# The squares of both feature halves summed on GpSimd before the first norm's product, and ring loads and first gathers reordered

## The chip, the cores and the metric

The kernel runs on one core of one Trainium2 chip. The metric is the device time in microseconds (us) of one execution. PE is the matrix engine (TensorE), DVE the vector engine, ACT the scalar engine, POOL the GpSimd engine, and SP the engine that issues most DMAs. Each engine runs its own instructions in order; they meet at semaphores.

## The reference

4096 tokens (64 sequences of 64 tokens, 256 features) go through a conditioned adapter, attention with a window inside each sequence, and a layer of 32 experts, of which each token takes the best 4:

```
def _rmsnorm(x, w):
    rms = rsqrt(mean(x * x, axis=-1) + 1e-5)
    return w * (x * rms)
x0 = up(relu(down(x, cond)), cond) + x          # per-sequence adapter
qkv = _rmsnorm(x0, attn_norm_w) @ qkv_w + qkv_b # 16 query heads, 4 key heads of 64
x2 = x0 + attention(rope(q), rope(k), v) @ proj_w + proj_b
h2 = _rmsnorm(x2, ffn_norm_w)
topv, topi = top_k(h2 @ gate_w + gate_b, 4); gw = softmax(topv)
y2 = sum over the 4 experts of gw * ((silu(g) * u) @ W_down),  [u, g] = h2 @ W_up
out = x + x2 + y2
```

## The kernel before

Part 1 handles the tokens in eight chunks of 512 (numbered m = 0 to 7), with tokens along the free axis and the 256 features as two halves (c = 0, 1) of 128 partitions. Part 2 handles 159 tiles of 128 token-expert pairs, expert by expert. Each engine's order in part 1 is written out by hand in the table ORDERS: a start, then one text for chunk 0, one for chunks 1 to 6, one for the last. A word there is one step; `steps_of` unrolls them.

The steps of one chunk that matter here, in order:

- `up` on DVE (L1411, L1414) scales two products out of PSUM; `up` on POOL (L683, L689) adds them and the input, which gives the chunk's activations x0 in two halves; `up` on ACT (L1125) squares each half into a scratch tile, tmp[0][0] and tmp[0][1].
- `sums` on PE (L808) multiplies each squared half with a matrix of ones and accumulates both products in one PSUM bank, which leaves the sum over all 256 features in every row. ACT turns it into an inverse root (L1157, L1159), DVE multiplies x0 with it (L1469) and splits the result into an upper and a lower part (L1473).
- `pair` (five a chunk) makes query and key heads: PE L821, DVE L1486, then on POOL one subtraction and one addition (L706, L708). DVE may not write the products of a pair before POOL has finished the pair two before it.
- `split` (96 in all, twelve in most chunks) prepares the experts' weights for part 2: a third of an expert is loaded by SP (L537, L539), ACT rounds it to an upper part (L1245), POOL subtracts that to get the lower part (L724), SP stores both (L546, L547). Five buffers hold thirds, three hold upper parts.
- Routing of the chunk before: DVE picks the experts (`route_list`, L1587 to L1606, with the small product L1596 in it), ACT packs and tags rows (L1229, L1237), and `put` on POOL scatters 128 rows into an expert's list by an indirect DMA (L717).

In chunks 1 to 6 POOL's order is: four splits, a pair, three splits, two pairs, a split, two pairs, two splits, eight puts, `up`, split, put, split, seven puts.

Between the parts SP loads the first four experts into a ring of four slots (`load_expert`, L604): the first when the last stores have landed, three more when the last projection of part 1 is done. ACT waits until every put has landed, loads the first tile's rows (`load_rows`, L1328), reads the plan of the tiles, loads the rows of five more tiles, and then begins the tiles (`turn_in`, L1296). PE keeps itself busy with products that nobody reads (`unread`, L764), whose numbers stand in BUSY: 30 before the plan's small products, 40 after them. Then PE turns the rows of tile 0 and tile 1 (L1008) and starts the experts' products (L1034).

Of the kernel before, what the change touches and what calls it, by code (L numbers as in the profile page):

```python
# [55 lines left out]

ROWS_AHEAD = NG - 4
NPUT, NLATE = 2, 4
BUSY = (11, 14, 24, 14, 20, 30, 40)


NP = 4
# [10 lines left out]

ORDERS = {
    "PE": ("""
        cond down up sums pair pair pair pair pair down score up value
    """, """
        value score turn_prob score attend sums project turn_prob pair pair score attend value pair
        project value pair turn_prob pair attend down value project turn_prob score attend up
        project  # L80
    """, """
        score route_turn score turn_prob route_turn value attend sums route_turn project turn_prob
        route_turn pair pair route_pick score attend value pair route_count project pair pair value
        turn_prob value attend down project turn_prob score attend up project
    """, """
        score route_turn score turn_prob route_turn route_pick attend route_turn value project
        route_count route_turn turn_prob attend route_turn route_pick value project route_count
        turn_prob route_turn score attend value route_pick project turn_prob attend route_count
        route_turn project route_pick route_turn route_pick route_count route_count
    """),  # L90
    "DVE": ("""
        cond down relu scale up weights apply pair pair pair pair pair constants down relu softmax_a
        up softmax_b value
    """, """
        value softmax_a softmax_b apply project softmax_a pair pair softmax_b softmax_a value pair
        value project pair pair softmax_b down relu value project softmax_a up softmax_b project
    """, """
        softmax_a softmax_a value softmax_b apply project softmax_b pair pair route_pick value
        softmax_a pair route_count project pair pair value route_list value softmax_b down project
        relu softmax_a up softmax_b project  # L100
    """, """
        softmax_a softmax_a route_pick value softmax_b project route_count route_list softmax_b
        route_pick project value route_count route_list softmax_a value softmax_b project route_pick
        route_count route_list project route_pick route_count route_list route_pick route_count
        route_list
    """),
    "ACT": ("""
        cond split split down split split weights up sums apply split split split down split split
        softmax_a up
    """, """  # L110
        turn_prob split softmax_a attend split sums split split apply project split turn_prob split
        split softmax_a split attend split split turn_prob softmax_a project split attend split down
        turn_prob split project split attend split softmax_a split split project up split
    """, """
        route_turn turn_prob route_turn softmax_a attend split sums split route_turn apply softmax_a
        project turn_prob split root route_turn pack split split attend split split split project
        split route_pick pack split turn_prob softmax_a attend tag tag turn_prob down project attend
        softmax_a split split pack tag up project tag pack
    """, """
        route_turn turn_prob route_turn root softmax_a attend route_pick pack route_turn softmax_a  # L120
        root route_turn turn_prob pack tag attend pack pack project route_pick route_turn tag
        project root route_turn turn_prob tag attend softmax_a tag pack turn_prob pack route_pick
        project attend tag route_turn root project route_turn root tag route_pick pack route_pick
        pack tag tag
    """),
    "POOL": ("""
        split split split split pair split pair pair up pair pair split split split split up
    """, """
        split split split split split split split pair split split pair split pair pair pair split
        split split split split up split split split  # L130
    """, """
        split split split split pair split split split pair pair split pair pair split split put put
        put put put put put put up split put split put put put put put put put
    """, """
        put put put put put put put put put put put put put put put put put put put put put put put
        put put put put put put put
    """),
    "SP": ("""
        load_third load_x_t load_third load_middle load_third store_third store_third load_third
        store_third load_third load_third load_late load_third store_third move store_third load_x_t  # L140
        move move move move load_third store_third load_third load_third store_third load_third
        store_third store_third load_third
    """, """
        load_third load_x_t store_third load_third store_third store_third load_third load_third
        store_third store_third store_third load_third store_third load_third move load_third move
        store_third fill_before load_third load_third store_x2 store_third store_third move move
        load_third store_x2 load_third load_third move store_third store_third store_third
        store_third load_third load_third load_third store_third load_third store_x2 store_third
        load_third store_x2 store_third load_third store_third
    """, """  # L150
        load_third load_x_t store_third load_third store_third load_third store_third store_third
        load_third fill_before move load_third store_third load_third store_x2 store_third move
        store_third load_third move move store_x2 load_third move store_third load_third store_third
        load_third store_x2 store_third store_x2 load_third store_third load_third store_third
    """, """
        store_x2 store_x2 fill_before store_x2 store_x2
    """),
}

# [11 lines left out]


GROUPS = len(ROOTS)
TIMES = {"cond": 1, "scale": 1, "weights": 1, "constants": 1, "load_middle": 1, "load_late": 1, "fill_before": NM, "down": NM, "relu": NM, "up": NM, "sums": NM, "apply": NM, "pair": NM * NPAIR,
         "move": NM * NPAIR, "load_x_t": NM, "root": GROUPS, "route_pick": GROUPS, "route_count": GROUPS,
         "route_list": GROUPS, "put": NT * TOPK, "split": 3 * E, "load_third": 3 * E, "store_third": 3 * E}

# [68 lines left out]
def program(nc, d):  # L246
# [7 lines left out]
    def sem(name):  # L254
        return ctx.enter_context(nc.semaphore(name))
# [50 lines left out]
    ones = sb1("ones", [P, P])  # L306
# [15 lines left out]
    tmp = [[spare[:, 4 * i + j, :] for j in range(4)] for i in range(2)]  # L322
# [35 lines left out]
    start = prob[1][:, :, :].rearrange("p a k -> p (a k)")  # L358
# [65 lines left out]
    ident_b = ident[:, :].bitcast(BF16)[:, 0:P]  # L424

    s_vector = sem("s_vector")


    s_early, s_middle, s_late, s_fill, s_before = (sem(f"s_{n}") for n in ("early", "middle", "late", "fill", "before"))
# [76 lines left out]
    def listed(t):  # L506

        return s_listed[put_at[t]], 16 * TOPK * put_at[:t + 1].count(put_at[t])
# [8 lines left out]
    def sync_program(e):  # L517
# [99 lines left out]

        w.wait_ge(s_q_add, NPAIR * NM)
        w.wait_ge(s_proj, NT)
        for n in range(1, RING):  # L620
            load_expert(n)

# [39 lines left out]
    def gpsimd_program(e):  # L662
# [13 lines left out]
        def up(m):  # L676
# [49 lines left out]
        for name, k in steps_of("POOL"):  # L726
            if name == "up":
                up(k)
            elif name == "pair":
# [22 lines left out]
    def tensor_program(e):  # L752
# [349 lines left out]
    def scalar_program(e):  # L1102
# [794 lines left out]
```

## Time and profile before

| what | value |
|---|---|
| runs | 982.19, 980.65, 976.25 us (median 980.65) |
| profiled execution | 978.0 us |
| its span, first to last instruction | 976.0 us |
| mean granted TensorE clock | 0.979 |

The profile is of one execution: its instructions fill 976.0 us, and 2.0 us lie around them. A row gives a start in us from the span's beginning, a duration in us, an engine and a line of the kernel; a remark in square brackets at its end is the idle time before it and who ended it.

### The profile page before, as it was taken

What the parts mean: (1) busy time and instruction counts of PE and PEld (TensorE: products, weight loads), DVE (VectorE), ACT (ScalarE), POOL (GpSimd) and SP (SyncE); (2) the same over time, 40 slices, a digit from 0 to 9 for tenths busy, and PEclk for the clock granted to TensorE, in tenths of its full rate; (3) what the DMA queues carried; (4) which work ended last, traced back from release to release, by engine and by line L of the source; (5) the groups of instructions that cost most, each with busy time, mean ns of one, the idle gap of its engine ahead of it and who ended that gap; (6) DMA issues with size and microseconds to landing.
All of it is one profiled execution on the core that took longest, in us unless ns stands there. A gap on an engine that the chain in (4) does not pass through costs nothing.

```text
span 976.0 us, 21879 instructions
## 1 busy us (share of the span) xinstructions
PE 921.6 (94%) x7434; PEld 742.7 (76%) x7434; DVE 804.2 (82%) x1808; ACT 523.1 (54%) x1246; POOL 542.5 (56%) x507
## 2 busy tenths in 40 slices
PE   7989899989999999898988999999999999999998
PEld 3657676776867678676753888888888888888887
DVE  5989799999999989998864777777777877777777
ACT  3144463836557374573750666665666666566641
POOL 3647558897888778787565233433343334343340
PEclk9989999999999899999998999999999999999999
DMA  8789889798897978879249877777867759663798
GB/s 276 195 258 306 277 260 288 242 303 264 278 306 242 291 242 286 253 264 276 92 147 347 269 246 278 246 252 253 285 218 284 256 188 317 232 231 108 249 394 303
DMA packets 127447, 251.41 MB, mean 258 GB/s; under 512 B 18756, under 2 KB 66122, under 8 KB 126797
## 3 DMA queue, kind: packets, MB, share of 16 engines
q1 hardware_dynamic: 83436, 186.79, 57.8%
q0 software_dynamic: 13776, 34.64, 9.8%
q10 hardware_dynamic: 30128, 28.58, 9.6%
q8 instruction: 64, 1.05, 0.5%
q14 instruction: 43, 0.34, 0.1%
HBM read 135.64 MB, written 102.12 MB: 244 GB/s over the span
## 4 chain that ended last, share of the span: by engine, by line
PE 57%; DVE 15%; POOL 9%; issue 6%; DMA 5%; ACT 4%; SPq 3%; ACTq 0%; DVEq 0%; POOLq 0%
PE gbank L1034 11%; PE scores L1034 11%; PE scores L1053 5%; PE gbank L1053 5%; DVE ring L1486 5%; PE gbank L904 5%; POOL lists L717 5%; DMA rows_in<-lists 2%; PE gbank L1097 2%; PE gbank L821 2%; DVE entry L1596 2%; PE scores L1008 2%; PE gbank L1008 2%; PE gbank L1043 2%; PE scores L1043 2%
## 5 line engine op out<-in xcount | busy, mean ns | idle before, releaser
L739 POOL DMA_INDIRECT pick_rows<-rows_out,pair_i x159 | 158.7, 998 | 265.6 <-ACT rows_out L1310 262.2
L724 POOL TENSOR_TENSOR ring<-ring 128x512 fp32r<-128x512 f32 x96 | 123.5, 1297 | 64.1 <-ACT ring L1245 63.8
L717 POOL DMA_INDIRECT lists<-put_rows,slot_i x112 | 108.8, 972 | 54.8 <-issue 29.8
L1034 PE MATMUL scores<-ring,in_part 128*128 x480 | 132.6, 412 | 1.5 <-DVE in_part L1726 1.5
L1034 PE MATMUL gbank<-ring,in_part 128*128 x474 | 129.8, 409 | 0.0
L821 PE MATMUL gbank<-h_t,w_qk 128*128 128x512 f32 x480 | 117.8, 399 | 1.6 <-ACT ring L1189 0.7
L904 PE MATMUL gbank<-w_o,ring 128*128 128x256 f32 x512 | 116.5, 381 | 1.8 <-ACT ring L1189 1.7
L1245 ACT ACTIVATE ring<-ring 128x512 fp32r<-128x512 f32 x96 | 59.5, 627 | 108.9 <-DMA w_parts<-ring 74.6
L1486 DVE SCALAR_TENSOR_TENSOR ring<-gbank,b_qk,rope 128x512 f32<-128x512 f32 x160 | 107.9, 743 | 3.8 <-PE gbank L821 3.5
L904 PEld LDWEIGHTS gbank<-w_o,ring 128*128 128x128 f32 x512 | 95.2, 191 | 14.2 <-ACT ring L1189 2.7
L821 PEld LDWEIGHTS gbank<-h_t,w_qk 128*128 128x128 f32 x480 | 88.8, 188 | 22.6 <-ACT ring L1189 1.1
L1034 PEld LDWEIGHTS scores<-ring,in_part 128*128 128x128 f32 x480 | 85.0, 191 | 15.8 <-issue 1.7
L1034 PEld LDWEIGHTS gbank<-ring,in_part 128*128 128x128 f32 x474 | 83.2, 189 | 13.7
L1053 PEld LDWEIGHTS scores<-ring,mid_part 128*128 128x128 f32 x480 | 67.8, 189 | 7.8 <-issue 0.4
L1053 PEld LDWEIGHTS gbank<-ring,mid_part 128*128 128x128 f32 x474 | 67.0, 189 | 7.2
L1296 ACT ACTIVATE in_part<-scores,norm_w 128x128 fp32r<-128x128 f32 x160 | 50.0, 364 | 39.4 <-PE scores L1008 23.1
L1053 PE MATMUL scores<-ring,mid_part 128*128 x480 | 70.2, 282 | 0.1
L1053 PE MATMUL gbank<-ring,mid_part 128*128 x474 | 69.2, 282 | 0.0
L1734 DVE SCALAR_TENSOR_TENSOR mid<-scores,rows_in,silu 128x256 f32<-128x256 f32 x80 | 38.6, 483 | 35.3 <-ACT silu L1302 35.3
L1302 ACT ACTIVATE silu<-scores,rows_in 128x256 f32<-128x256 f32 x80 | 37.9, 473 | 51.5 <-PE scores L1034 51.2
L1734 DVE SCALAR_TENSOR_TENSOR mid<-gbank,rows_in,silu 128x256 f32<-128x256 f32 x79 | 38.1, 482 | 27.4 <-ACT silu L1302 27.4
L1302 ACT ACTIVATE silu<-gbank,rows_in 128x256 f32<-128x256 f32 x79 | 37.4, 474 | 42.1 <-PE gbank L1034 41.2
(214 smaller groups left out, 1930.2 us busy)
## 6 DMA issues: line engine op xcount, KB each, us to landing
w_parts<-ring SPq DMA_DIRECT2D x192, 256.0 KB, 4.0
ring<-w_parts SPq DMA_DIRECT2D x32, 1536.0 KB, 7.7
rows_in<-lists ACTq DMA_DIRECT2D x159, 136.0 KB, 3.8
ring<-in_W_up SPq DMA_DIRECT2D x64, 256.0 KB, 4.4
picks<-pick_rows SPq DMA_DIRECT2D x6, 2048.0 KB, 13.9
ring<-in_W_down SPq DMA_DIRECT2D x32, 256.0 KB, 4.3
q_r<-rot SPq DMA_DIRECT2D x16, 512.0 KB, 6.4
q_r<-ring SPq DMA_DIRECT2D x16, 512.0 KB, 6.7
```

What stands on the lines that cost most here:

```text
L717: e.indirect_dma_start(out=lists, out_offset=bass.IndirectOffsetOnAxis(ap=slot_i[r % NPAY][:, s * TOPK + k:s * TOPK + k + 1], axis=0), in_ ...
L724: e.tensor_tensor(lower, lower.bitcast(F32), upper.bitcast(F32), ALU.subtract).then_inc(s_lower, 1)
L739: e.indirect_dma_start(out=pick_rows, out_offset=bass.IndirectOffsetOnAxis(ap=pair_i[:, i:i + 1], axis=0), in_=rows_out[i % NY][:, :], in_ ...
L821: ins = e.matmul(bank[:, :], w_qk[:, x, c, 2 * j + o, :], h_t[i][:, y, c, :], start=k == 0, stop=k == len(CHUNK_PRODUCTS) - 1)
L904: ins = e.matmul(bank[:, 0:D], y_t[:, n // REP, n % REP, :, :].rearrange("p b s -> p (b s)"), w_o[:, n, :], start=False, stop=n == 2 * REP ...
L1034: ins = e.matmul(front[i % FRONTS], in_parts[i % IN_BUFS][x][:, c, :], ring[:, bass.ds(at + y * WE + c * 2 * DFF, 2 * DFF)], start=k == 0, ...
L1053: ins = e.matmul(out, mid_parts[i % 2][x][:, c, :], ring[:, bass.ds(at + y * WE + KC * 2 * DFF + c * D, D)], start=k == 0, stop=k == len(C ...
L1245: e.activation(w_upper[q % NU], w_third[q % NW].bitcast(F32), ACT.Copy).then_inc(s_upper, 1)
L1296: ins = e.activation(in_parts[i % IN_BUFS][0][:, c, :], front[i % FRONTS][:, c * P:(c + 1) * P], ACT.Copy, scale=norm2_w[:, c:c + 1])
L1302: e.activation(silu[i % 2][:, :], front[i % FRONTS][:, DFF:2 * DFF], ACT.Silu, scale=rows_in[i % NG][:, D + 2:D + 3]).then_inc(s_silu, 1)
L1486: e.scalar_tensor_tensor(out=by_seq(t[n][:, :]), in0=by_seq(gbank[banks[o]][:, :]), scalar=b_qk[:, 2 * j + o:2 * j + o + 1], in1=rope[:, t ...
L1734: e.scalar_tensor_tensor(out=mid[i % MID_BUFS][:, :], in0=front[i % FRONTS][:, 0:DFF], scalar=rows_in[i % NG][:, D + 2:D + 3], in1=silu[i ...
```

## The change

Four edits:

1. A new POOL step `squares` adds tmp[0][1] to tmp[0][0] once ACT has squared both halves, for chunks 1 to 7. PE's `sums` then makes one product of the sum where it made two; chunk 0 stays as it was.
2. POOL's order gets the step: right behind `up` of chunk 1; behind `up`, split, split of chunk 2; behind `up`, split, put of chunks 3 to 7 (ahead of a split and seven puts). No other word of ORDERS changes; the other lines of the table are only wrapped anew.
3. SP waits for the landing of every put before it loads experts 1 to 3 into the ring.
4. ACT begins tile 0 (`turn_in(0)`) before it loads the rows of tiles 4 and 5, where it loaded all five first. PE's unread products before the plan are 20 where they were 30.

```diff
-BUSY = (11, 14, 24, 14, 20, 30, 40)
+BUSY = (11, 14, 24, 14, 20, 20, 40)
...
     "POOL": ("""
-        split split split split pair split pair pair up pair pair split split split split split up
+                 split split split split pair split pair pair up pair pair squares split split split split split up
+        squares
     """, """
...
-        split split split split up split split split split
+        split split split split up split split squares split
     """, """
...
-        put put put put put put up split put split put put put put put put put
+        put put put put put put up split put squares split put put put put put put put
...
         w.wait_ge(s_proj, NT)
+        for t in sorted(max(u for u in range(NT) if put_at[u] == b) for b in range(NPUT + NLATE)):
+            w.wait_ge(*listed(t))
         for n in range(1, RING):
             load_expert(n)
...
+        def squares(m):
+            if m == 0:
+                return
+            w.wait_ge(s_sq, KC * (m + 1))
+            e.tensor_tensor(tmp[0][0][:, :], tmp[0][0][:, :], tmp[0][1][:, :], ALU.add).then_inc(s_sq_sum, 1)
...
-            for c in range(KC):
-                w.wait_ge(s_sq, KC * m + c + 1)
-
-                ins = e.matmul(bank[:, :], ones[:, :], tmp[0][c][:, :], start=c == 0, stop=c == KC - 1)
+            if m == 0:
+                for c in range(KC):
+                    w.wait_ge(s_sq, c + 1)
+                    ins = e.matmul(bank[:, :], ones[:, :], tmp[0][c][:, :], start=c == 0, stop=c == KC - 1)
+            else:
+                w.wait_ge(s_sq_sum, m)
+                ins = e.matmul(bank[:, :], ones[:, :], tmp[0][0][:, :], start=True, stop=True)
             ins.then_inc(s_ssq1, 1)
...
         for i in range(AHEAD, ROWS_AHEAD):
+            if i == ROWS_AHEAD - 2:
+                turn_in(0)
             load_rows(i)
-        turn_in(0)
         turn_in(1)
```

(AHEAD is 1 and ROWS_AHEAD is 6, so tile 0 is begun between the row loads of tiles 3 and 4.)

## Rows read from the trace of the kernel before

**Rows 1.** The page: share of the chain that ended last, by engine.

```profile
PE 57%; DVE 15%; POOL 9%; issue 6%; DMA 5%; ACT 4%; SPq 3%; ACTq 0%; DVEq 0%; POOLq 0%
```

**Rows 2.** The timeline around the sums of chunk 3: start, duration, engine, line.

```profile
179.81 0.63 ACT L1125 ACTIVATE ring<-x_t 128x512 f32<-128x512 f32 x1 [0.62 <-POOL x_t L689]
...
182.18 1.29 POOL L724 TENSOR_TENSOR ring<-ring 128x512 fp32r<-128x512 f32 x1
...
184.21 1.99 PE L808 MATMUL gbank<-ring,ones 128*128 128x512 f32 x4
```

**Rows 3.** The timeline of the rest of the same stage, until chunk 4's step up.

```profile
202.66 1.30 POOL L724 TENSOR_TENSOR ring<-ring 128x512 fp32r<-128x512 f32 x1 [0.97 <-ACT ring L1245]
...
215.65 4.35 DVE L1596 TENSOR_TENSOR entry<-gexp,gsum 128x16 f32<-128x16 f32 x1
...
217.46 2.49 POOL L724 TENSOR_TENSOR ring<-ring 128x512 fp32r<-128x512 f32 x2
...
222.57 0.98 POOL L717 DMA_INDIRECT lists<-put_rows,slot_i  x1 [2.62 <-ACT put_rows L1237]
...
232.51 2.50 POOL L683 TENSOR_TENSOR ring<-ring 128x512 f32<-128x512 f32 x2
```

**Rows 4.** All executions of DVE's L1596: shortest, median, longest in ns.

```profile
L1596 DVE TENSOR_TENSOR entry<-gexp,gsum x11: 167/3792/4704, 157.3 to 514.9; 128x16 f32<-128x16 f32 x6, 128x8 f32<-128x8 f32 x3, 128x4 f32<-128x4 f32 x2
```

**Rows 5.** SP's queue in the stage of chunk 3, and what it waited for.

```profile
SPq L546 <- POOL ring L724: 9.6, 3, 7.5
```

**Rows 6.** The chain that ended last, in the stage of chunk 5.

```profile
308.19 1.32 POOL ring L724
309.52 0.33 SPq L546
...
328.15 4.27 DMA ring<-in_W_up
```

**Rows 7.** Groups on POOL by line: busy us, mean ns; idle before, and who ended it.

```profile
L683 POOL TENSOR_TENSOR ring<-ring 128x512 f32<-128x512 f32 x14 | 17.5, 1273 | 3.6 <-DVE ring L1414 3.3
```

**Rows 8.** POOL's timeline behind the step up of chunks 1 and 2.

```profile
67.11 1.26 POOL L724 TENSOR_TENSOR ring<-ring 128x512 fp32r<-128x512 f32 x1 [2.23 <-ACT ring L1245]
...
127.79 1.27 POOL L724 TENSOR_TENSOR ring<-ring 128x512 fp32r<-128x512 f32 x1 [1.84 <-ACT ring L1245]
```

**Rows 9.** A window in the stage of chunk 5: length, busy us of PE, PEld, DVE, ACT, POOL, clock, DMA.

```profile
335.00:340.00 5.00, 5.00 (x18) 2.06 (x11) 4.76 (x9) 1.71 (x6) 2.07 (x3) 0.50 1.03 269
```

**Rows 10.** POOL's timeline in the stage of chunk 5, at its end.

```profile
350.68 2.50 POOL L683 TENSOR_TENSOR ring<-ring 128x512 f32<-128x512 f32 x2 [2.37 <-DVE ring L1414]
```

**Rows 11.** The chain that ended last, between the parts.

```profile
527.38 5.49 DMA lists<-put_rows,slot_i
532.96 0.33 ACTq L1328
```

**Rows 12.** Landing of all puts (L717), in us: shortest, median, longest.

```profile
DMA to landing us min/median/max: 2.4/3.2/7.2
```

**Rows 13.** Landing of all row loads (L1328), likewise.

```profile
DMA to landing us min/median/max: 2.1/3.8/7.4
```

**Rows 14.** The timeline between the parts: SP, PE and ACT.

```profile
509.52 9.16 SPq L604 DMA_DIRECT2D ring<-w_parts  x4
...
514.63 8.29 PE L764 MATMUL scores<-ident 128*128 128x512 bf16 x30 [0.60 <-DVE filled L1581]
...
535.78 0.44 PE L1008 MATMUL scores<-ident,rows_in 128*128 128x128 f32 x2 [2.62 <-DMA rows_in<-lists]
...
536.75 1.14 ACT L1296 ACTIVATE in_part<-scores,norm_w 128x128 fp32r<-128x128 f32 x4 [20.73 <-PE scores L1008]
...
538.40 2.85 PE L1034 MATMUL scores<-ring,in_part 128*128 x6 [1.50 <-DVE in_part L1726]
```

**Rows 15.** Landing of the ring loads (L604), likewise.

```profile
DMA to landing us min/median/max: 7.2/7.7/16.8
```

**Rows 16.** The scatters of the tiles' results (L739): count, first and last start.

```profile
L739 POOL DMA_INDIRECT pick_rows<-rows_out,pair_i x159: 982/983/1957, 549.2 to 951.2; - x159
```

More of the change, by code:

```diff
@@ L75 @@
     "PE": ("""
-        cond down up sums pair pair pair pair pair down score up value
+                 cond down up sums pair pair pair pair pair down score up value
     """, """
-        value score turn_prob score attend sums project turn_prob pair pair score attend value pair
-        project value pair turn_prob pair attend down value project turn_prob score attend up
-        project
+                 value score turn_prob score attend sums project turn_prob pair pair score attend
+        value pair         project value pair turn_prob pair attend down value project turn_prob
@@ L81 @@
+        score attend up         project
     """, """
-        score route_turn score turn_prob route_turn value attend sums route_turn project turn_prob
-        route_turn pair pair route_pick score attend value pair route_count project pair pair value
-        turn_prob value attend down project turn_prob score attend up project
+                 score route_turn score turn_prob route_turn value attend sums route_turn project
+        turn_prob         route_turn pair pair route_pick score attend value pair route_count
@@ L85 @@
+        project pair pair value         turn_prob value attend down project turn_prob score attend
+        up project
     """, """
[L86 to L89, printed above, removed]
+                 score route_turn score turn_prob route_turn route_pick attend route_turn value
@@ L90 @@
+        project         route_count route_turn turn_prob attend route_turn route_pick value project
+        route_count         turn_prob route_turn score attend value route_pick project turn_prob
+        attend route_count         route_turn project route_pick route_turn route_pick route_count
+        route_count
     """),
     "DVE": ("""
-        cond down relu scale up weights apply pair pair pair pair pair constants down relu softmax_a
-        up softmax_b value
+                 cond down relu scale up weights apply pair pair pair pair pair constants down relu
@@ L106 @@
+        route_pick route_count         route_list
     """),
     "ACT": ("""
-        cond split split down split split weights up sums apply split split split down split split
-        softmax_a up
+                 cond split split down split split weights up sums apply split split split down
+        split split         softmax_a up
     """, """
-        turn_prob split softmax_a attend split sums split split apply project split turn_prob split
-        split softmax_a split attend split split turn_prob softmax_a project split attend split down
@@ L113 @@
-        turn_prob split project split attend split softmax_a split split project up split
+                 turn_prob split softmax_a attend split sums split split apply project split
+        turn_prob split         split softmax_a split attend split split turn_prob softmax_a project
+        split attend split down         turn_prob split project split attend split softmax_a split
+        split project up split
     """, """
-        route_turn turn_prob route_turn softmax_a attend split sums split route_turn apply softmax_a
@@ L116 @@
-        project turn_prob split root route_turn pack split split attend split split split project
-        split route_pick pack split turn_prob softmax_a attend tag tag turn_prob down project attend
-        softmax_a split split pack tag up project tag pack
+                 route_turn turn_prob route_turn softmax_a attend split sums split route_turn apply
+        softmax_a         project turn_prob split root route_turn pack split split attend split
+        split split project         split route_pick pack split turn_prob softmax_a attend tag tag
@@ L119 @@
+        turn_prob down project attend         softmax_a split split pack tag up project tag pack
     """, """
[L120 to L123, printed above, removed]
@@ L124 @@
-        pack tag tag
+                 route_turn turn_prob route_turn root softmax_a attend route_pick pack route_turn
+        softmax_a         root route_turn turn_prob pack tag attend pack pack project route_pick
+        route_turn tag         project root route_turn turn_prob tag attend softmax_a tag pack
+        turn_prob pack route_pick         project attend tag route_turn root project route_turn root
+        tag route_pick pack route_pick         pack tag tag
     """),
     "POOL": ("""
-        split split split split pair split pair pair up pair pair split split split split up
+        split split split split pair split pair pair up pair pair squares split split split split up
@@ L138 @@
     "SP": ("""
[L139 to L142, printed above, removed]
+                 load_third load_x_t load_third load_middle load_third store_third store_third
+        load_third         store_third load_third load_third load_late load_third store_third move
@@ L143 @@
+        store_third load_x_t         move move move move load_third store_third load_third
+        load_third store_third load_third         store_third store_third load_third
     """, """
[L144 to L147, printed above, removed]
@@ L148 @@
-        store_third load_third load_third load_third store_third load_third store_x2 store_third
-        load_third store_x2 store_third load_third store_third
-    """, """
[L151 to L154, printed above, removed]
+                 load_third load_x_t store_third load_third store_third store_third load_third
@@ new lines @@
+        load_third         store_third store_third store_third load_third store_third load_third
+        move load_third move         store_third fill_before load_third load_third store_x2
+        store_third store_third move move         load_third store_x2 load_third load_third move
+        store_third store_third store_third         store_third load_third load_third load_third
+        store_third load_third store_x2 store_third         load_third store_x2 store_third
+        load_third store_third
@@ L155 @@
+    """, """
+                 load_third load_x_t store_third load_third store_third load_third store_third
+        store_third         load_third fill_before move load_third store_third load_third store_x2
+        store_third move         store_third load_third move move store_x2 load_third move
+        store_third load_third store_third         load_third store_x2 store_third store_x2
+        load_third store_third load_third store_third
     """, """
-        store_x2 store_x2 fill_before store_x2 store_x2
+                 store_x2 store_x2 fill_before store_x2 store_x2
@@ L173 @@
 GROUPS = len(ROOTS)
-TIMES = {"cond": 1, "scale": 1, "weights": 1, "constants": 1, "load_middle": 1, "load_late": 1, "fill_before": NM, "down": NM, "relu": NM, "up": NM, "sums": NM, "apply": NM, "pair": NM * NPAIR,
+TIMES = {"cond": 1, "scale": 1, "weights": 1, "constants": 1, "load_middle": 1, "load_late": 1, "fill_before": NM, "down": NM, "relu": NM, "up": NM, "squares": NM, "sums": NM, "apply": NM, "pair": NM * NPAIR,
          "move": NM * NPAIR, "load_x_t": NM, "root": GROUPS, "route_pick": GROUPS, "route_count": GROUPS,
@@ L728, in gpsimd_program @@
                 up(k)
+            elif name == "squares":
+                squares(k)
             elif name == "pair":
```

21 lines of the change are left out of this document (11 added, 10 removed).

## The prediction, as it was written before the change was run

> **What bounds the kernel now.** I read the page first, for the chain that ended last by engine [rows 1]. PE has 57% of it, but part 2 is nearly all PE, and the change is in part 1 and in the seam between the parts. So the question goes to the stages of part 1, to the timeline of one of them.
>
> Take the stage of chunk 3. ACT ends the second square at 180.44, and PE makes the two products of the sum from 184.21 for 1.99 us [rows 2]. PE's product is waited for by ACT, DVE and the pairs, so at first sight the sum lies on the path. The end of the stage tells another story. DVE starts the small product L1596 at 215.65 and needs 4.35 us for 16 numbers a partition [rows 3]; over all eleven executions the shortest took 0.17 us and the median 3.79 [rows 4]. It ends at 220.00, and POOL's last two splits, which start at 217.46 and take 2.49, end at 219.95 [rows 3]. DVE stood there until POOL was through with a row of tensor instructions. Its result makes the slots, the slots make the tags, and only then does the first put go out, at 222.57, after POOL had idled 2.62 [rows 3]. Eight puts later POOL starts chunk 4's `up` at 232.51 [rows 3]. So the end of POOL's splits is what sets the next stage, through DVE's wait.
>
> SP confirms it from another side: it waited 9.6 us in the stage, in three waits, for POOL's split before it could store a third [rows 5]. In the stage of chunk 5 the chain that ended last itself runs POOL's split at 308.19, SP's store at 309.52, and through SP's queue to a load of weights at 328.15 [rows 6]. POOL comes first in both forms of the loop. The loop in words: puts, `up`, split, put, split, seven puts, splits and pairs, L1596, slots, puts.
>
> **The change part by part: PE's product.** One of two fp32 products goes in seven chunks. Two took 1.99 us [rows 2], so each saves 1.0, and 7 x 1.0 = 7.0 us of PE's work. What it is worth: PE, ACT's logarithm and exponential, DVE's normalised halves and the pairs come 1.0 earlier in each stage. DVE then reaches L1596 1.0 sooner and stands there 1.0 longer, because POOL ends it. I count 0; the bound on the other side is the full -7.0.
>
> **The change part by part: POOL's addition.** It has the shape of L683, 128x512 fp32 in and out, with a mean of 1.27 us [rows 7]. Chunk 1: ACT's second square is done about when the next split's upper part is awaited; POOL idled 2.23 us ahead of that split [rows 8], so the addition fits. Chunk 2: POOL idled 1.84 ahead of the split that comes second behind it [rows 8]; it fits too. If that cover is gone, each costs up to 1.27.
>
> Chunks 3 to 7: the addition takes the place of the split at 182.18 [rows 2]. Both squares are there (180.44), so POOL doesn't wait. It ends near 183.45, and PE comes at 184.21, so PE doesn't wait either, with 0.7 us to spare. But behind it in POOL's queue stand a split, seven puts, nine splits or so and all pairs of the stage, and all are 1.27 later. SP's stores hang on those splits, the next loads on the stores, and ACT's upper parts on the loads. POOL's small gaps, such as 0.97 ahead of a split that waited for ACT [rows 3], are thus made by POOL's own delay of half a stage before, and move with it. So I take the full 1.27 in each of five chunks: 5 x 1.27 = +6.35. Ends: 0, if the gaps take it up, and as calculated; a wider one, of the clock, is the third rival.
>
> A GpSimd addition might also hold DVE up where it lies. In the trace DVE stands still for 4.35 us beside POOL's tensor instructions [rows 3]. The Trainium skill ("SBUF — State Buffer", Who interferes with whom) says why: GpSimd and a DVE instruction with two inputs in SBUF share a port, which whoever starts first holds for that instruction while the other blocks. By that rule L1596 would get in when the POOL instruction then running ends, about 1.3 us after its start, and the end of POOL's row of splits would gate nothing; here it waited through at least three POOL instructions, and the measurement decides. The second rival below is what the rule's plain reading gives.
>
> **The change part by part: the seam.** The last put starts at 527.38 and lands 5.49 later [rows 11]; meanwhile the ring loads that SP issued from 509.52 on are in the DMA engines [rows 14]. With three of them held back it should land like the median put, 3.2 [rows 12]: -2.3. Ends: the shortest, 2.4, gives -3.1; if the loads are not what delays it, 0. Then SP and ACT are released together, and the three ring loads run against the first row loads. Tile 0's rows were issued at 532.96 [rows 11] and used at 535.78 [rows 14], which is 2.8; the median row load of part 2, with weights being loaded beside it, takes 3.8 and the longest 7.4 [rows 13]. I take the median: +1.0 (ends 0 and +4.6). ACT begins tile 0 ahead of two row loads: PE had turned the rows by 536.22 and ACT began at 536.75 [rows 14], so -0.5. Sum: -2.3 + 1.0 - 0.5 = -1.8, between -3.6 and +4.6.
>
> The row loads of tiles 4 and 5, put behind `turn_in(0)`, go out about a microsecond later than they did, and are needed some 7 us after the first product; nothing. The ring loads themselves: at 7.7 each [rows 15], one after another from 530.6, they land at 538, 546 and 554. The 159 tiles take (951.2 - 549.2) / 158 = 2.54 us each [rows 16], five to an expert, so the second expert is wanted near 549, the fourth near 575. Hidden; had they to wait for one another twice as long, the second would still be in time. Behind those loads on SP stand the loads for the residuals and expert 4, which come some 12 us later and are wanted after 585. Ten fewer unread products: thirty took 8.29 [rows 14], so the plan comes about 2 us sooner; but ACT needs the plan only when the puts have landed, so 0. The second batch then also ends 2 us sooner, as do the rows, so PE idles as long as before ahead of its first product; 0, at the worst the first group's 2.85 us [rows 14] is not cut.
>
> **Sum.** +6.35 - 1.8 = +4.55 us. Against the profiled execution, 978.0: 982.5. That execution and the three runs are four draws, 976.25, 978.0, 980.65 and 982.19, with a mean of 979.3; the profiled one stands 2.65 below the median of the three. I put the forecast on the mean: 979.3 + 4.55 = 983.8.
>
> **Rivals.** First, POOL's gaps take up the addition: if the splits behind the puts are paced by DMA transfers that started earlier, not by POOL, the addition is free, and only the seam is left: 979.3 - 1.8 = 977.5. For it speaks the 0.97 gap [rows 3]; against it SP's long waits for POOL [rows 5]. Second, the sum on PE is the bound: L1596 gets in between two POOL instructions, POOL's end stops mattering, and all seven products come off: 979.3 - 7.0 - 1.8 = 970.5. Against it speaks the median of 3.79 us [rows 4].
>
> Third, and slower: PE now has 1.0 less to do in a stage that is 1.27 longer, so it idles longer ahead of the attention products at a stage's end, which wait for ACT behind its splits. In the stage of chunk 5 the clock was granted at 0.50 from 335 to 340 [rows 9], the lower of its two levels, 1.2 GHz, after PE had idled; PE's chain then came after POOL's, and POOL waited 2.37 for DVE [rows 10]. If chunks 3, 4 and 6 get that too, it adds 3 x 2.37 = 7.1: 979.3 + 4.55 + 7.1 = 991.0. It decides from the point where that idle stretch lengthens enough for the lower level to last through the next products. Fourth, the first two row loads take the longest time, 7.4, beside the ring loads: +6.35 - 2.3 - 0.5 + 4.6 = +8.15, 987.4.
>
> **How the numbers follow.** Forecast 0.48, first rival 0.17, second 0.12, third 0.13, fourth 0.10. The range leaves out the second rival and the upper part of the third: from the first with the seam's better end (975.7) and the spread of the runs to just short of the third, 974 to 990. One per cent, 9.8 us, is about what a measurement of this kernel can tell from no change. Faster by that takes the second rival in full, at 970.5 on the edge: 0.06. Slower takes the third, at 991.0 just past the edge, or a sum of smaller losses: 0.08. The same: 0.86.
>
> **What would show it.** In the profile after: PE's L808 half as long in seven chunks; a POOL addition of about 1.27 behind chunk 3's first put with PE never waiting for it; the distance from one chunk's sums to the next longer by 1.27; L1596 still ending with POOL's last split, and longer than before. If the stages keep their length, POOL was not the loop; if they shorten, PE was. In the seam: the last put landing about 3 us after its start, and the first row load no faster than before. Wrong would be, above all, that the addition changes which instructions DVE and POOL block each other in, or that DMA sets the pace of the splits.

## The result, and the profile after

| | before | after |
|---|---|---|
| median of five runs, us | 979.89 | 988.45 |
| range, us | 976.25 to 982.19 | 987.62 to 989.39 |
| profiled execution, us | 978.0 | 987.62 |
| its span, us | 976.0 | 985.8 |

The change makes the kernel slower: the ratio is 1.0107, with a 95% interval of 1.0074 to 1.0139, which is 10.5 us (7.3 to 13.6); the medians lie 8.56 us apart. The forecast was a loss of 4.55, at 983.8; the median after is 4.65 above that. One execution of 2305.89 us, of the run below that holds the ring loads back without the squares, is left out of its ratio.

The chain that ended last, by engine, tells where to look: DMA has 9% of it, where it had 5% [rows 1], and DVE 10% for 15%.

```profile
PE 55%; DVE 10%; DMA 9%; POOL 9%; issue 6%; ACT 6%; SPq 4%; ACTq 0%; DVEq 0%; POOLq 0%
```

**The sum itself** went as the change says. Below, the addition is L705 and PE's product L829; POOL's split is now L740, its put L733, `up` L693 and L699. First the group of the addition, then the timeline around the sums of chunk 3, which answers to [rows 2].

```profile
L705 POOL TENSOR_TENSOR ring<-ring x7: 1272/1287/1297, 65.2 to 421.3; 128x512 f32<-128x512 f32 x7
its engine sat idle before it (us, times) until:
  ACT ring L1146: 0.7, 1
who waited for it (us, times):
  PE gbank L829: 0.3, 1
```

```profile
178.88 1.30 POOL L705 TENSOR_TENSOR ring<-ring 128x512 f32<-128x512 f32 x1
180.12 1.27 POOL L740 TENSOR_TENSOR ring<-ring 128x512 fp32r<-128x512 f32 x1
...
180.90 1.12 PE L829 MATMUL gbank<-ring,ones 128*128 128x512 f32 x2
```

The addition takes 1.29 us, PE's sum 1.12 where it took 1.99 [rows 2], and PE stood still for POOL once in seven chunks, for 0.3 us. The sum itself thus costs nothing that was lost.

**The stages of part 1** show where that goes. The last put of part 1 starts at 533.42, against 527.38 [rows 11]: 6.04 later. POOL begins `up` of chunk 3 at 171.47 and of chunk 4 at 232.82, where it began them at 174.77 and 232.51 [rows 3]: chunk 2 gained 3.3 and chunk 3 lost 3.6. These rows say where (DVE's L1618 was L1596 [rows 4]).

```profile
156.66 0.19 DVE L1618 TENSOR_TENSOR entry<-gexp,gsum 128x16 f32<-128x16 f32 x1
```

```profile
213.02 1.32 POOL L722 TENSOR_TENSOR ring<-ring 128x512 f32<-128x512 f32 x1
213.20 4.85 DVE L1618 TENSOR_TENSOR entry<-gexp,gsum 128x16 f32<-128x16 f32 x1
215.47 2.53 POOL L740 TENSOR_TENSOR ring<-ring 128x512 fp32r<-128x512 f32 x2
...
216.46 1.98 PE L910 MATMUL gbank<-ring,v_s 64*64 64x256 f32 x16 [2.89 <-ACT ring L1202]
...
218.37 3.78 PE L801 MATMUL gbank<-x_t,w_down_ones 128*128 128x512 f32 x4
...
232.82 1.27 POOL L693 TENSOR_TENSOR ring<-ring 128x512 f32<-128x512 f32 x1 [2.35 <-DVE ring L1436]
```

In chunk 2 the small product slipped in between POOL's instructions and took 0.19 us instead of 4.65. In chunk 3 it waited until 218.05, when POOL's splits ended (218.00), as before. But PE idled 2.89 for ACT, its next products ran at a low clock, and POOL then waited 2.35 for DVE, a wait that [rows 3] does not have; with the 1.29 of the addition that is the 3.6. The windows of that place (length, busy us of PE, PEld, DVE, ACT, POOL, clock, DMA share, GB/s) give the clock; in the kernel before both read 1.00.

```profile
215.00:220.00 5.00, 3.54 (x18) 1.63 (x19) 4.93 (x6) 4.07 (x10) 3.00 (x3) 0.57 0.99 265
220.00:225.00 5.00, 5.00 (x17) 3.33 (x16) 4.67 (x7) 0.00 (x0) 3.46 (x4) 0.75 0.98 282
```

**The seam** is where the forecast has the wrong sign. From the chain that ended last, the timeline and the windows after the last put (L1349 loads rows, L1029 turns them, L1055 are the experts' first products):

```profile
533.42 2.42 DMA lists<-put_rows,slot_i
535.95 0.39 ACTq L1349
...
538.37 10.77 DMA rows_in<-lists
549.18 0.69 PE gbank L1029 x2
```

```profile
541.30 0.44 PE L1029 MATMUL scores<-ident,rows_in 128*128 128x128 f32 x2 [3.09 <-DMA rows_in<-lists]
544.37 0.69 PE L1029 MATMUL scores<-ident,rows_in 128*128 128x128 f32 x2 [2.62 <-DMA rows_in<-lists]
544.71 2.91 PE L1055 MATMUL scores<-ring,in_part 128*128 x6
...
549.18 0.69 PE L1029 MATMUL gbank<-ident,rows_in 128*128 128x128 f32 x2 [1.14 <-DMA rows_in<-lists]
```

```profile
535.00:540.00 5.00, 3.22 (x15) 1.27 (x13) 0.00 (x0) 0.00 (x0) 0.00 (x0) 1.00 0.59 204
540.00:545.00 5.00, 1.07 (x5) 0.84 (x6) 0.68 (x3) 0.63 (x2) 0.00 (x0) 0.84 1.03 419
545.00:550.00 5.00, 3.86 (x12) 2.77 (x11) 1.84 (x7) 3.06 (x7) 0.00 (x0) 0.50 1.03 404
```

The put lands in 2.42 us, not 5.49 [rows 11]: that part worked. The first rows, issued at 535.95, are used at 541.30, 5.35 later, where 2.8 was read from [rows 11, 14]. A later row load takes 10.77 in the chain; by its landing the longest has 10.0, where it had 7.4 [rows 13]. With the three ring loads under way the DMA engines are full from 540 to 550: a share of 1.03 and 419 and 404 GB/s. PE is busy 1.07 of 5 us, and the clock then falls to 0.50, the lower level. In the kernel before the ring loads had their heavy stretch ahead of the row loads: 354 GB/s from 530 to 535, then 144 and 138 while the first rows came.

```profile
530.00:535.00 5.00, 3.16 (x15) 1.25 (x13) 0.00 (x0) 0.00 (x0) 0.00 (x0) 1.00 0.89 354
535.00:540.00 5.00, 2.48 (x8) 1.72 (x9) 1.26 (x6) 2.42 (x5) 0.00 (x0) 0.85 0.53 144
540.00:545.00 5.00, 5.00 (x23) 4.06 (x23) 2.70 (x10) 2.69 (x8) 0.00 (x0) 0.81 0.43 138
```

A measure for the seam that can be taken in every run: the time from the last put's start to the scatter of the twentieth tile, when all tiles come evenly. Before it is 597.59 - 527.38 = 70.21, after 607.10 - 533.42 = 73.68: +3.47. With +6.04 in part 1 that is 9.5 of the 9.8 us between the two spans.

```profile
597.59 0.98 POOL L739 DMA_INDIRECT pick_rows<-rows_out,pair_i  x1 [1.56 <-ACT rows_out L1310]
```

```profile
607.10 0.98 POOL L757 DMA_INDIRECT pick_rows<-rows_out,pair_i  x1 [1.56 <-ACT rows_out L1331]
```

### The profile page after: what moved, and what is told of

Same layout as the page of the kernel before. It is cut to its first block, busy times and chain, and to the rows that moved or that the text cites. A ratio compares the mean times of both kernels' runs of the same rounds, so it can differ in the third digit from the quotient of the medians.

```text
span 985.8 us, 21841 instructions
## 1 busy us (share of the span) xinstructions
PE 921.1 (93%) x7410; PEld 739.9 (75%) x7410; DVE 801.7 (81%) x1808; ACT 523.2 (53%) x1246; POOL 553.8 (56%) x514
## 3 DMA queue, kind: packets, MB, share of 16 engines
q8 instruction: 64, 1.05, 0.4%
## 4 chain that ended last, share of the span: by engine, by line
PE 55%; DVE 10%; DMA 9%; POOL 9%; issue 6%; ACT 6%; SPq 4%; ACTq 0%; DVEq 0%; POOLq 0%
PE gbank L1055 11%; PE scores L1055 10%; PE gbank L1074 5%; PE scores L1074 5%; PE gbank L925 5%; DMA rows_in<-lists 4%; POOL lists L733 4%; DVE ring L1508 3%; DMA ring<-in_W_up 2%; PE gbank L1118 2%; DMA w_parts<-ring 2%; PE gbank L842 2%; PE scores L1029 2%; POOL ring L740 2%; PE gbank L910 2%
## 5 line engine op out<-in xcount | busy, mean ns | idle before, releaser
L740 POOL TENSOR_TENSOR ring<-ring 128x512 fp32r<-128x512 f32 x96 | 125.7, 1321 | 56.4 <-ACT ring L1266 56.0
L733 POOL DMA_INDIRECT lists<-put_rows,slot_i x112 | 108.7, 971 | 54.0 <-issue 29.8
L1055 PE MATMUL scores<-ring,in_part 128*128 x480 | 133.8, 414 | 0.0
L1055 PE MATMUL gbank<-ring,in_part 128*128 x474 | 130.1, 409 | 0.0
L1055 PEld LDWEIGHTS scores<-ring,in_part 128*128 128x128 f32 x480 | 85.8, 192 | 14.4
L1055 PEld LDWEIGHTS gbank<-ring,in_part 128*128 128x128 f32 x474 | 83.5, 189 | 13.8
```

Source lines behind the costliest of these rows:

```text
L733: e.indirect_dma_start(out=lists, out_offset=bass.IndirectOffsetOnAxis(ap=slot_i[r % NPAY][:, s * TOPK + k:s * TOPK + k + 1], axis=0), in_ ...
L740: e.tensor_tensor(lower, lower.bitcast(F32), upper.bitcast(F32), ALU.subtract).then_inc(s_lower, 1)
L1055: ins = e.matmul(front[i % FRONTS], in_parts[i % IN_BUFS][x][:, c, :], ring[:, bass.ds(at + y * WE + c * 2 * DFF, 2 * DFF)], start=k == 0, ...
```

## The experiments

Two theories stood after the result. Mine: the squares cost about 6 us in part 1, and the seam loses because row loads and ring loads collide. The rival: the seam gains as forecast, and part 1 alone carries the loss. Every run below was timed against the kernel before on the same chip, whose medians there were 978.3 to 979.6. The figures are ratios to it, with a 95% interval in brackets; a ratio of 0.001 is 0.98 us.

**The seam without the squares.**

```diff
+BUSY: 20 for 30
+SP: for t in <last tile of each put buffer>: w.wait_ge(*listed(t))   # ahead of experts 1 to 3
+ACT: turn_in(0) ahead of load_rows(4)
```

> The kernel before with the seam's edits alone (SP waits for every put before ring loads 1 to 3, tile 0 begun between the row loads, 20 unread products), and no addition on GpSimd. My theory after the result: released together, the ring loads and the first row loads run against each other, so tiles 0 to 3 start late: about +3.5 us over the kernel before, with tile 4 some 3.5 us later after the last put's issue. The forecast's own term says -1.8 us. A third theory, that the whole loss is in part 1, says 0.

Measured: 1.0017 [0.9988, 1.0045], so +1.7 us with an interval from -1.2 to +4.4. In its trace the put lands in 2.43, the first rows take 5.44, a later row load 9.72, and the twentieth scatter comes 72.95 after the last put. The forecast's gain of 1.8 isn't there. The time alone can't tell +1.7 from 0; the traces together can: the three runs with SP's wait and no later ring loads lie at 72.95 to 74.02, the five with the old seam at 70.21 to 71.93 (the table below).

```profile
524.29 2.43 DMA lists<-put_rows,slot_i
...
526.82 5.44 DMA rows_in<-lists
...
532.91 9.72 DMA rows_in<-lists
```

**The squares without the seam.** Edits 1 and 2 of the change alone.

> The kernel before with GpSimd's addition and the single product on PE, and the old seam. My theory: part 1 is a loop through GpSimd, so about +6 us (five chunks of 1.27, less or more by 3 where DVE's small product slips in or the clock falls). If the loss is all in the seam: 0. If PE's product were the bound: -7.

Measured: 1.0059 [1.0029, 1.0090], +5.8 us (+2.8 to +8.8).

**The addition alone.** As the last run, but the sum goes to a tile that nobody reads; PE waits for it and still makes both products.

```diff
+e.tensor_tensor(tmp[0][3][:, :], tmp[0][0][:, :], tmp[0][1][:, :], ALU.add).then_inc(s_sq_sum, 1)
 # sums, m > 0:
+w.wait_ge(s_sq_sum, m)
```

> The kernel before with GpSimd's addition into a spare tile, waited for by PE, which still makes both products; old seam. The addition's result is not used. If GpSimd's place in the loop is the cost: the same as with the single product, +6 us, within 1.5 of it. If what costs is that PE has less to do and its clock falls: near 0. If PE's product is worth its time: 7 us above the run with the single product.

Measured: 1.0061 [1.0030, 1.0091], +6.0 us. In its trace PE's idle time ahead of the sums never names POOL. So the cost comes with the addition on POOL, and the product that PE saves buys nothing that shows.

**One product, no addition.** PE makes one product of the first half's squares in chunks 1 to 7; the second half's squares are left out of the sum.

> The kernel before where PE makes one product for the norm's sum in chunks 1 to 7 and nobody adds the other half: the second half's squares are left out of the sum, so the values differ. Old seam, no addition on GpSimd. If part 1 hangs on GpSimd: 0, between -1.5 and +1.5. If it hangs on PE: -7. If less work on PE lowers its clock: +2 to +5.

Measured: 0.9987 [0.9959, 1.0015], between -4.0 and +1.5 us. The full -7.0 is excluded.

**The addition twice.** PE waits for the first only; DVE's later normalising step waits for the second, which has long been done.

```diff
+e.tensor_tensor(tmp[0][3][:, :], tmp[0][0][:, :], tmp[0][1][:, :], ALU.add).then_inc(s_sq_sum, 1)
+w.wait_ge(s_sq_sum, 2 * m - 1)
+e.tensor_tensor(tmp[0][3][:, :], tmp[0][0][:, :], tmp[0][1][:, :], ALU.add).then_inc(s_sq_sum, 1)
```

> The kernel before with POOL's addition made twice in each of chunks 1 to 7, into a tile that nobody reads; PE keeps both products and waits for the first addition alone, as in the run with one addition that cost 6.2 (ratio 1.0061). The old seam. Theory (POOL's time is the loop of the stages, and each 1.27 us laid on it in chunks 3 to 7 comes back in full): 5 x 2.54 = 12.7, and 0.3 + 0.7 in chunks 1 and 2, where POOL's gaps are 2.23 and 1.84 wide: 13 to 14 us over the kernel before, ratio 1.013 to 1.014. Rival 1 (the cost of one addition was the wait and the shifted order, not its length): no more than with one, ratio 1.006. Rival 2 (gaps of POOL take up the second): ratio 1.008 to 1.010.

Measured: 1.0148 [1.0105, 1.0190], +14.5 us (+10.3 to +18.6) for 13 to 14 expected. Twice the time on POOL costs about twice as much, though PE waits for the first addition only and the order is the same: it is POOL's time that costs, not the wait or the new order. Both rivals lie below the interval, the second only just.

**The seam's edits one by one, and the collision taken away.** The second run has SP's wait alone, the third ACT's order and the 20 unread products alone. The first and the fourth hold the ring loads back until the first six row loads have landed too, without and with the squares:

```diff
 for t in <last tile of each put buffer>: w.wait_ge(*listed(t))
+for i in range(ROWS_AHEAD):
+    w.wait_ge(s_rows_in[i], 16)
 for n in range(1, RING):
     load_expert(n)
```

> The kernel before with the changed seam (SP's wait for the puts, ACT's new order, 20 unread products), and one wait more: SP holds ring loads 1 to 3 back until the first six row loads have landed as well. No addition of squares. Theory (the loss is the collision of row loads with ring loads): with the collision gone the first row load takes about 2.4 us instead of 5.4, the last put still lands in about 2.4, and tile 4 starts some 18 to 19 us after the last put's issue (20.9 in the kernel before, 23.0 with the changed seam alone): 2 to 3 us under the kernel before, ratio 0.997 to 0.998. Rival 1 (the row loads are slow for a reason of their own): tile 4 stays at 23 us, ratio about 1.002. Rival 2 (the ring loads, some 3 us later, come too late for the second expert): a wait of PE's of several us shows near tile 6.

> The kernel before with SP's wait for all puts alone; ACT's order and the 30 unread products as before. Theory: the wait alone makes the collision, so tile 4 starts about 23 us after the last put's issue, ratio 1.002 to 1.004. Rival (ACT's order, with tile 0 begun ahead of two row loads, does the harm): 19 to 20 us, ratio 0.998 to 0.999, from the put that lands 3 us sooner.

> The kernel before with ACT's order and the 20 unread products alone; SP loads the ring as before. Theory: worth nothing or half a microsecond, tile 4 at 20.4 to 20.9 us after the last put's issue, ratio 0.9995 to 1.000. Rival (fewer unread products let TensorE's clock fall to its lower level before tile 0): tile 4 one to three us later, ratio 1.001 to 1.003.

> The whole change, with ring loads 1 to 3 held back until the first six row loads have landed too. Theory (two costs that add up: +6 of the squares in part 1, and a seam that gains 2 to 3 once the row loads run alone): 3 to 4 us over the kernel before, ratio 1.003 to 1.004, and tile 4 some 18 to 19 us after the last put's issue. Rival (what the whole change costs above the squares' +6 lies in part 1, not in the seam): 8 us over the kernel before, ratio 1.008 or more.

Measured, in this order: 0.9972 [0.9941, 1.0002], 1.0037 [1.0013, 1.0061], 0.9979 [0.9951, 1.0007] and 1.0065 [1.0036, 1.0094]. SP's wait alone is slower than the kernel before, and the only seam edit whose interval excludes 1. The expectations speak of tile 4: its products start 18.16, 24.40, 20.69 and 16.43 us after the last put's start, against 20.68 before and 23.00 with the seam alone.

In the run with SP's wait alone the put lands early and the rows come late, with ACT's old order and all 30 unread products (L1330 loads rows there). Its first row loads took 5.5 to 13.2 us to land, 11.0 in the median; the six of the kernel before took 2.6 to 2.8.

```profile
529.67 2.43 DMA lists<-put_rows,slot_i
532.20 0.39 ACTq L1330
...
534.64 10.90 DMA rows_in<-lists
```

With the row loads ahead of the ring loads the loss is gone. The rows of the first of the four runs show it (there L1332 loads rows and L1012 turns them): the first rows come 2.1 after their issue, and the long row load is now one of a later tile, after which PE idles only 1.34.

```profile
525.10 2.42 DMA lists<-put_rows,slot_i
527.61 0.34 ACTq L1332
...
534.84 8.17 DMA rows_in<-lists
```

```profile
529.71 0.44 PE L1012 MATMUL scores<-ident,rows_in 128*128 128x128 f32 x2 [0.86 <-DMA rows_in<-lists]
...
543.05 0.44 PE L1012 MATMUL gbank<-ident,rows_in 128*128 128x128 f32 x2 [1.34 <-DMA rows_in<-lists]
```

The fourth run came out at +6.4, about what the squares cost alone, where 3 to 4 was expected. Its interval, +3.5 to +9.2, holds 4 and the rival's 8 alike, so its time doesn't decide between them. Its seam has 66.56 to the twentieth scatter, but PE then waits 1.89 for rows at 620.89, and by the fortieth tile the distance is 121.12, where the five with the old seam have 121.40 to 123.32. Most of what its seam gained over those was given back there; why is open.

**One ring load early, two late.** Expert 1 as early as before, experts 2 and 3 after the first six row loads.

> The kernel before with ACT's new order and 20 unread products, expert 1 loaded into the ring as early as in the kernel before, and experts 2 and 3 only when all puts and the first six row loads have landed. No addition of squares. Theory (a ring load in the DMA engines delays whatever lands beside it, puts and row loads alike): one early ring load is through before the last put, so the put lands in about 2.4 to 3 us and tile 0's and tile 1's rows in 2.4; the scatter of tile 20 starts 67 to 69 us after the last put's issue (70.2 in the kernel before, 69.2 with all three loads late); 2 to 4 us under the kernel before, ratio 0.996 to 0.998. Rival (the two late loads only push the collision to the rows of tiles 6 to 10, and what was gained is given back there): tile 20 at 70 or later, ratio 0.999 to 1.000.

Measured: 0.9975 [0.9946, 1.0005], with 68.55 to the twentieth scatter. Three seams without the collision (0.9972, 0.9979, 0.9975) are each about 2.5 us under the kernel before, and each interval still holds 1: no version is shown to beat it.

**All runs, by the two measures of the traces** (one execution each):

| run | last put starts | to the twentieth scatter |
|---|---|---|
| before | 527.38 | 70.21 |
| seam only | 524.29 | 72.95 |
| SP's wait only | 529.67 | 74.02 |
| ACT's order only | 519.16 | 70.33 |
| seam, ring late | 525.10 | 69.15 |
| seam, one ring load early | 525.11 | 68.55 |
| one product | 529.45 | 71.87 |
| squares only | 531.54 | 71.93 |
| addition only | 528.81 | 71.48 |
| addition twice | 539.78 | 71.41 |
| after | 533.42 | 73.68 |
| after, ring late | 535.70 | 66.56 |

The six with part 1 untouched begin the last put at 525.1 in the mean (519.16 to 529.67), the four with one addition at 532.4 (528.81 to 535.70): +7.3. The three with SP's wait and nothing that delays the ring loads further have 73.55 to the twentieth scatter, the five with the old seam 71.38: +2.2. Together 9.5, inside the ratio's 7.3 to 13.6.

## Why the prediction was wrong

**The step that failed is the seam's term, -1.8.** Its put was right: -2.3 was forecast and -3.07 came, the better end. What it set against that was too small: "I take the median: +1.0 (ends 0 and +4.6)". That prices one row load, tile 0's, whose rows came 2.5 us later after their issue than before. But PE turns the rows of tile 1 as well before its first product, and those came 3 us behind tile 0's. So the products of tile 0 start 11.29 us after the last put's start, where they started 11.02 after it [rows 11, 14]: the put's gain is gone by then. The rest of the loss lies behind the first product, where the sum has nothing: PE waits 1.14 for tile 3's rows, the clock is at 0.50 from 545 to 550, and the first scatter comes 25.34 after the last put's start instead of 21.80. The other two runs with SP's wait and early ring loads agree: tile 0's products at 11.37 and 11.41 (the five with the old seam: 11.48 in the mean), and waits of 1.15 and 1.17 for tile 3's rows.

The median of all row loads was the wrong row to take. Most of them run beside one expert's load at a time: such a load lands in 7.7 us [rows 15], and five tiles take 12.7. Here three loads of 1.5 MB are issued within a microsecond and a half of the first row loads. The fourth rival had the mechanism and nearly the price, -2.3 - 0.5 + 4.6 = +1.8, against +2.2 in the traces and +1.7 and +3.6 timed, and its 987.4 lies 1.05 us from the median after. That nearness is in part luck: it lays 4.6 on the first row loads, of which the first cost 2.5, and nothing on what came behind. I gave it 0.10, because I priced a collision that I had seen coming with a row from a stretch that has none like it. That the wait alone makes the loss is settled by the run with SP's wait alone.

**Part 1's term, +6.35, was right in size**: +5.8 and +6.0 timed, 7.3 in the traces. That POOL's time closes the loop held, and the doubled addition bears it out. The first rival falls: POOL's gaps don't take the addition up behind the puts. In chunks 1 and 2 they did: the 2.23 and 1.84 us of idle time before [rows 8] have shrunk by the length of the addition, to 0.74 and 0.22 in chunk 1,

```profile
65.25 1.27 POOL L705 TENSOR_TENSOR ring<-ring 128x512 f32<-128x512 f32 x1 [0.74 <-ACT ring L1146]
66.74 1.27 POOL L740 TENSOR_TENSOR ring<-ring 128x512 fp32r<-128x512 f32 x1 [0.22 <-ACT ring L1266]
```

and to 0.61 in chunk 2.

```profile
127.40 1.27 POOL L740 TENSOR_TENSOR ring<-ring 128x512 fp32r<-128x512 f32 x1 [0.61 <-ACT ring L1266]
```

But the evenness, 1.27 in each of five chunks, was not right. From `up` of chunk 3 to `up` of chunk 7 the six executions without an addition and with both products took 233.9 us in the mean and the four with one addition 241.8: 2.0 a stage. Up to chunk 3 the latter were 1.35 sooner, and behind chunk 7 only 0.7 later. The extra 0.7 a stage stands in POOL's waits for DVE at `up` of chunks 4 to 7, 4.1 us in the mean of the four against 1.1 in that of the six: 4.7 in the kernel after, 5.5 in the run with squares only, but 1.1 in that with the addition only, whose four stages took 238.2, or 1.07 more each.

Two things stand ahead of such waits. One is the third rival's: in chunk 3 of the profiled execution PE idles, the clock falls (0.57 from 215 to 220), and POOL waits 2.35, about the 2.37 of that rival; in chunks 4 and 6 it does not. That the clock is the cause is read from the rows; no run varied it. The other is that DVE's small product gets in early. In chunk 5 it took 3.98 to 5.08 us in the seven executions without an addition and 0.32 to 2.38 in the five with one or two. Eight times in chunks 3 to 6 of the twelve executions it took 2.4 us or less, and each time POOL waited 1.1 to 2.4 for DVE at the next `up`. Those eight stages last 61.1 us in the mean, the other sixteen of the same executions 60.1. So an early end of DVE's wait does not start the next stage sooner: that POOL's time comes back in full is shown, but not that it comes back through L1596, as the prediction has it. By which path it does is open. How the 0.7 divides is open too; on medians the runs with and without PE's second product, +5.8 and +6.0, do not differ.

**PE's product was worth nothing that shows**, as counted: -1.3 with an interval from -4.0 to +1.5. The second rival at 970.5 falls with it. But its mechanism, L1596 getting in between POOL's instructions, does happen: 0.19 in chunk 2 after, and in chunk 5 a middle course:

```profile
334.50 2.38 DVE L1618 TENSOR_TENSOR entry<-gexp,gsum 128x16 f32<-128x16 f32 x1
```

```profile
335.57 3.03 POOL L740 TENSOR_TENSOR ring<-ring 128x512 fp32r<-128x512 f32 x2
```

It ended at 336.88, about when the first of the two splits did, and the DVE work behind it ran on beside the second; it had stood through that split and through the POOL instruction that ran when it began. In chunk 3 it stood through four POOL instructions from 213.02 on, one of them begun ahead of it. In chunk 2 it began at 156.66, as one POOL instruction ended and the next began, and got in at once. The Trainium skill ("SBUF — State Buffer", Who interferes with whom) has the lock held for one instruction; the trace agrees in chunk 2 and differs in chunks 3 and 5, so the rule doesn't say which it will be.

**Of what would show it**: the shorter product, PE not waiting and the put at about 3 us came as written. "The first row load no faster than before" was the seam's point, and it was 2.5 us slower. L1596 did not always end with POOL's last split, and the distance between stages grew by 2.0, not 1.27. Its last sign of being wrong, that the addition changes which instructions DVE and POOL block each other in, did appear, in chunk 5 of all five executions with an addition.

**The rest.** Ten fewer unread products and ACT's order were counted at -0.5; together they measured -2.1 [-4.8, +0.7], which neither bears this out nor speaks against it. In the profile after ACT begins tile 0 0.04 after its rows are turned, where it took 0.53, but PE then stands still for tile 1's rows. SP's waits of 9.6 us [rows 5] reach past the stage of chunk 3; between its bounds, 174.77 and 232.51, they are 8.8, which changes nothing. The base of 979.3 was right: 979.89 with five runs.

## What to carry to other kernels

A wait that holds transfers back moves their traffic to the moment when it is satisfied. Look at what else is released by the same event, and price all of it, not the first transfer alone, with rows from a stretch where the DMA engines are as full as they will be then. A transfer that is held back should wait for the small ones that the engines are waiting for, too. And an instruction handed from an engine with slack to the one that closes the loop cost about its duration, or more, in every stage without a gap, however little the other engine's saving was worth.

## What was unexpected

Executions of one part 1 differ widely: the last put starts between 519.16 and 529.67 in six kernels with the same part 1, and in chunk 2 of these the small DVE product takes 0.19 to 4.65 us for the same 16 numbers. A difference of 6 us is thus seen in medians of many runs, not in a pair of traces. And a 136 KB row load beside three ring loads landed after up to 10.0 us in the kernel after, and 13.2 with SP's wait alone, where the first one ahead of them was used 2.1 after its issue.
